# Pacing of the indirect gathers, the order of the small steps and the placing of adjacency units in a four-layer graph network

## The reference

```
h = relu(layernorm(x)); x = x + relu([h, adj @ h] @ W.T + b)                        # layer 0
h = relu(layernorm(x)); x = x + unit_rows(((adj + I) scaled by degrees) @ h @ W.T + b)   # layer 1
h = relu(layernorm(x)); x = x + gru(relu((adj @ h) @ W_msg.T + b_msg), h)           # layer 2
h = relu(layernorm(x))                                                              # layer 3
  z   = leaky_relu(lap_mul(adj, h) @ W1 + b1)
  S   = exp(-0.5 * sqrt(max(|z_i|^2 + |z_j|^2 - 2 z_i.z_j, 0) + 1e-10))
  S   = S on the four most similar j of each row i, else 0
  x   = x + lap_mul(S + adj, h) @ W2 + b2
lap_mul(A, x) = d * (A @ (d * x)),  d = 1 / sqrt(row sums of A)
```

## Time and profile before

| | |
|---|---|
| median of 3 runs | 1389.42 us (1389.1 to 1389.64) |
| the profiled execution, its own time | 1390.72 us |
| its span, first to last instruction | 1388.9 us |
| PE busy | 1312.7 us (95%) |
| DVE busy | 1120.5 us (81%) |
| ACT busy | 867.8 us (62%) |
| POOL busy | 153.1 us (11%) |
| DMA, mean over the span | 222 GB/s |
| granted TensorE clock, mean | 0.98 |

### The profile page before, as it was taken

How to read it: one execution, slowest core, us unless ns; L and a number is a source line. 1 busy time by engine, 2 the same in 40 slices (tenths; PEclk the granted TensorE clock), 3 DMA queues, 4 the chain that set the end, 5 groups by cost and what they waited for, 6 DMA issues and landing times.

```text
span 1388.9 us, 15894 instructions
## 1 busy us (share of the span) xinstructions
PE 1312.7 (95%) x5542; PEld 981.8 (71%) x5542; DVE 1120.5 (81%) x1551; ACT 867.8 (62%) x1302; POOL 153.1 (11%) x178
## 2 busy tenths in 40 slices
PE   7999999999899989999999999999999999869697
PEld 4567888788688767778887778777777775435454
DVE  6898888898998888976658998599999997435455
ACT  5456765447666676765656777566666664547676
POOL 0000110000000000000001000000000001756562
PEclk9999999999999999999999999999999999979899
DMA  9799997558776775666557899201111115769886
GB/s 348 246 328 344 361 340 288 183 186 308 242 239 232 272 278 184 214 210 210 190 183 278 292 318 355 96 1 38 53 53 53 51 44 185 257 227 339 288 312 251
DMA packets 87471, 308.30 MB, mean 222 GB/s; under 512 B 11360, under 2 KB 11488, under 8 KB 87392
## 3 DMA queue, kind: packets, MB, share of 16 engines
q1 hardware_dynamic: 78048, 280.01, 57.6%
q0 software_dynamic: 9344, 27.27, 5.8%
HBM read 303.04 MB, written 4.19 MB: 221 GB/s over the span
## 4 chain that ended last, share of the span: by engine, by line
PE 66%; DVE 27%; issue 3%; ACT 2%; DMA 1%; another core or an unknown queue 1%; ACTq 0%; DVEq 0%
PE ps L507 15%; PE ps L509 15%; PE ps L508 15%; PE ps L512 12%; DVE best_at L1349 9%; DVE rows_T L1345 9%; DVE A_lo L1253 4%; PE ps L579 1%; PE ps L541 1%; PE ps L611 1%; PE ps L613 1%; PE ps L612 1%; DMA ring<-adj_t 1%; PE ps L565 1%
## 5 line engine op out<-in xcount | busy, mean ns | idle before, releaser
L744 ACT ACTIVATE A_hi<-ring 128x1024 fp32r<-128x1024 f32 x399 | 410.1, 1055 | 138.7 <-PE ps L509 82.0
L1253 DVE TENSOR_TENSOR A_lo<-ring,A_hi 128x1024 fp32r<-128x1024 f32 x354 | 416.6, 1217 | 5.9 <-ACT A_hi L744 5.7
L507 PE MATMUL ps<-A_hi,G_odd_hi 128*128 128x512 f32 x602 | 254.2, 422 | 15.8 <-DVE A_lo L1253 9.4
L508 PE MATMUL ps<-A_lo,G_odd_hi 128*128 128x512 f32 x602 | 237.0, 394 | 3.5 <-issue 3.5
L509 PE MATMUL ps<-A_hi,G_odd_lo 128*128 128x512 f32 x602 | 237.4, 394 | 1.9 <-issue 1.9
L507 PE MATMUL ps<-A_hi,G_even_hi 128*128 128x512 f32 x428 | 174.2, 407 | 2.6 <-DVE A_lo L1253 2.6
L744 ACT ACTIVATE scores<-ps,neg_sq 128x1024 f32<-128x1024 f32 x128 | 139.8, 1112 | 53.0 <-PE ps L701 52.4
L509 PE MATMUL ps<-A_hi,G_even_lo 128*128 128x512 f32 x428 | 167.1, 390 | 0.0
L508 PE MATMUL ps<-A_lo,G_even_hi 128*128 128x512 f32 x428 | 166.8, 390 | 0.0
L512 PE MATMUL ps<-ring,G_last 128*128 128x512 f32 x332 | 156.4, 601 | 6.3 <-issue 5.5
L507 PEld LDWEIGHTS ps<-A_hi,G_odd_hi 128*128 128x128 f32 x602 | 114.4, 190 | 56.0 <-issue 20.4
(11 more groups left out here) (156 smaller groups left out, 1650.0 us busy)
## 6 DMA issues: line engine op xcount, KB each, us to landing
ring<-adj_t SPq DMA_DIRECT2D x524, 512.0 KB
row_piece<-adj_rows POOLq DMA_DIRECT2D x32, 512.0 KB, 6.5
X<-x_rows SPq DMA_DIRECT2D x8, 256.0 KB, 7.9
scaled_rows<-G_last POOLq DMA_DIRECT2D x8, 256.0 KB, 2.7
landing<-scaled_rows,best_at POOLq DMA_INDIRECT x128
out_rows<-X SPq DMA_DIRECT2D x8, 256.0 KB, 8.6
pack<-packed SPq DMA_DIRECT2D x1, 836.0 KB, 14.5
pack<-packed SPq DMA_DIRECT2D x1, 192.0 KB, 3.8
```

What stands on the lines that cost most here:

```text
L507: mm(acc, G_hi[odd][:, kb, t, :], hi, start=start, stop=False)
L508: mm(acc, G_hi[odd][:, kb, t, :], lo, start=False, stop=False)
L744: return nc.scalar.activation(out_ap, in_ap, func, **k)
L1253: v_.tensor_tensor(A_lo[:, s, :, :], ring[:, s, :, :], hi, ALU.subtract).then_inc(lower_ready, 1)
```

## The change

Five edits, in `Plan`, the ScalarE, the VectorE and the GpSimd programs:

1. GpSimd no longer waits for `used` ahead of a tile's gathers. `scanned` and `weighted` stay.
2. ScalarE's small steps of block m - 1 stand later: `similarity` behind the third tile of block m instead of the first, `new_roots` behind the fourth instead of the second, `scale_last` behind the first tile of block m + 1 instead of the third of m. At the end of the search they are interleaved accordingly.
3. VectorE's `new_degrees` and `new_inverse` of the first block move one tile later; at the end `new_inverse` of the last but one block moves behind the values of tile 30, and `last_rest` moves from behind the places of tile 31 to behind those of tile 29.
4. Units stand beside seven of eight search tiles (9 to 15, 17 to 23, 25 to 30) instead of three of four (8 to 29): 20 instead of 17 ahead of tile 31, 14 instead of 17 beside tile 31, and the four of the operand block that is scaled last but one come behind those of block 2.
5. ScalarE enters the final stretch when 31 tiles are searched, and waits for the 32nd only at unit 6.

```diff
--- before.py
+++ after.py
@@ -70,10 +70,6 @@
 
 
 LAST_US, NEAR_US, NEAR_FIRST = 1.7, 5.37, 5.0
-
-
-
-UNITS_A_TILE, UNITS_AHEAD = 3.0, 16
 
 
 SPLIT_EVERY = 2
@@ -123,12 +119,16 @@
 
         ended = [b * HALVES + half for b in sorted(range(NB), key=lambda b: self.rank[3, b]) for half in range(HALVES)]
         self.beside = {}
-        for c in range(28):
+        for c in range(24):
             v = self.last_visit(c % 2, ended[c // 2], False)
-            at = 8 + c // 3 * 4 + c % 3
-            self.beside.setdefault(at if at < NT - 2 else NT - 1, []).append(v)
+            at = 9 + c * 8 // 7
+            self.beside.setdefault(min(at, NT - 1), []).append(v)
         for u in ended[:6]:
             self.beside[NT - 1].append(self.last_visit(2, u, False))
+        for c in range(24, 28):
+            v = self.last_visit(c % 2, ended[c // 2], False)
+            at = 9 + c * 8 // 7
+            self.beside.setdefault(min(at, NT - 1), []).append(v)
         self.search_end = len(self.visits)
         for b in range(2):
             for u in ended[-HALVES:]:
@@ -1021,29 +1021,33 @@
                     pair_out(TPB * m + k)
                     if 0 < TPB * m + k <= NB:
                         last_rows_out(TPB * m + k - 1)
-                    if k == 0 and m:
+                    if k == 0 and m > 1:
+                        scale_last(m - 2)
+                    elif k == 2 and m:
                         similarity(m - 1)
-                    elif k == 1 and m:
+                    elif k == 3 and m:
                         new_roots(m - 1)
-                    elif k == 2 and m:
-                        scale_last(m - 1)
             m = NB - 1
             act.wait_ge(negsq_ready, NB)
             pair_out(TPB * m)
+            scale_last(m - 2)
+            pair_out(TPB * m + 1)
+            pair_out(TPB * m + 2)
             similarity(m - 1)
-            pair_out(TPB * m + 1)
+            pair_out(TPB * m + 3)
             new_roots(m - 1)
-            pair_out(TPB * m + 2)
-            pair_out(TPB * m + 3)
             scale_last(m - 1)
             similarity(m)
             new_roots(m)
             scale_last(m)
 
-            act.wait_ge(scanned, NT)
+            act.wait_ge(scanned, NT - 1)
             for v in PLAN.visits[PLAN.search_end:]:
                 if v.split:
                     upper(v)
+                if v.n - PLAN.search_end == 6:
+
+                    act.wait_ge(scanned, NT)
                 if v.n - PLAN.search_end in (6, 10):
                     move_out(4, (v.n - PLAN.search_end) // 4 - 1)
                 elif v.b > 2 and v.u == 3:
@@ -1408,26 +1412,27 @@
                 scan(i)
                 if i % TPB == TPB - 1:
                     clamp(i // TPB)
-                elif i >= TPB and i % TPB == 0:
+                elif i >= TPB and i % TPB == (1 if i < 2 * TPB else 0):
                     new_degrees(i // TPB - 1)
-                elif i >= TPB and i % TPB == 1:
+                elif i >= TPB and i % TPB == (2 if i < 2 * TPB else 1):
                     new_inverse(i // TPB - 1)
 
 
             m = NB - 1
             scan_values(NT - 3)
+            scan_values(NT - 2)
             new_inverse(m - 1)
-            scan_values(NT - 2)
             scan_values(NT - 1)
             clamp(m)
             new_degrees(m)
             new_inverse(m)
-            for i in range(NT - 3, NT):
-                scan_places(i)
+            scan_places(NT - 3)
 
             dve.wait_ge(scanned, NT - 2)
             for k in range(NB):
                 last_rest(k)
+            scan_places(NT - 2)
+            scan_places(NT - 1)
             for v in PLAN.visits[PLAN.search_end:]:
                 if v.split:
                     lower(v)
@@ -1476,8 +1481,6 @@
                 pool.wait_ge(scanned, seek.index(t) + 1)
                 if t >= GSLOTS:
                     pool.wait_ge(weighted, t - GSLOTS + 1)
-                if t >= 2:
-                    pool.wait_ge(used, min(PLAN.search_end + int(UNITS_A_TILE * t) - UNITS_AHEAD, len(PLAN.visits)))
                 for r in range(TOPK):
                     pool.indirect_dma_start(
                         out=landing[:, k, r, :], out_offset=None, in_=scaled_rows,
```

## The result

| | before | changed |
|---|---|---|
| median, runs taken together | 1389.5 us | 1412.9 us (1408.2 to 1416.6) |
| ratio | | 1.016, 95% interval 1.014 to 1.019 |
| the profiled execution, its own time | 1390.7 us | 1413.65 us |
| its span | 1388.9 us | 1411.0 us |
| granted TensorE clock, mean | 0.98 | 0.97 |

The change costs 23 us, 1.6%. The forecast was 1385 and the range ended at 1400.

A forecast was written before the change was run, and what follows sets the result against it. VectorE was taken to bound the search, TensorE its end, with slow stretches during the gathers behind it. Terms -12 + 12 - 4 = -4 us took 1390.7 to 1386.7, less 1.3 over the median: 1385, range 1366 to 1400.

The forecast's parts named there:

- The place that bounds: Behind the search, 1209 to 1231 us: TensorE busy 5.7 of 22 us, almost everybody standing except GpSimd.
- Rival B: Slow stretches behind the search grow because the removed wait was a self-acting brake; +8, 1397 us; chance 0.27.
- Rival A: First slow stretch comes no earlier in TensorE's work, so the search's gain stays: 1377 us, or 1366; chance 0.29.
- Small steps: End of the search: VectorE's waits for scores of tiles 30 and 31 go, 4.7 us; first gather about 1171.
- Units beside seven of eight tiles: Search: still VectorE's bound, 3 units moved forward; first split about 1184 instead of 1196.3, 12 us gained.
- `last_rest`: Subtractions at the search's end move over the first gather: 2 of 4.2 us kept, continuous gathers from about 1173.
- No wait for `used`: First slow stretch: TensorE thins out at 1193, GpSimd goes on to tile 9, until 1223; 12 us handed back.
- 20 us of gathers: Behind the search: TensorE slows after some 16 gathers in a row (20 us), hence at 1193, unit 9 or so.
- the upper bound: First slow stretch: two more tiles of gathers get out, with `weighted` at four, 10 us more.
- Later stretches: Behind 1231 us: a third of GpSimd's breaks go; 4 of TensorE's 16.6 idle us taken as gained.
- Rival B's two signs: First slow stretch lasts past 1230; later breaks have TensorE under half busy for over 8 us each.
- a starved instruction stream: Slow stretch: would stay in its place of TensorE's program, also giving 1377; given 0.03 of the 0.29 chance.

## Why the prediction was wrong

**What was right.** The place that bounds, what happens in it, and the role of the wait: Rival B, "the removed wait was a brake that acts by itself", is what the runs with edit 1 alone and with edits 2 to 5 alone show on the first chip. Of Rival A half came true: its sign, a first stretch that "begins above 1200", did show (1205), and the stretch came "no earlier than before in TensorE's work", behind unit 12. Its price failed, since it took the length as given. That the stretch would take what edits 2 to 5 bring fits their ratio of 1.000 alone, in part by luck: there was little to take. With the wait in place their first split is at 1192.06, 4 us sooner than before, and `lower` of unit 19 at 1235.72, 1.9 us sooner.

**Small steps.** "In the steady search VectorE never waits for ScalarE, so nothing is gained there" was read for gain only. The new place of `similarity` asks for a lead of two tiles, and the rows from which the lead could be read, were taken for a local obstacle of `root`. Measured: -4.7 + 5.5 us; the first gather at 1175.85 instead of 1171.

**Units beside seven of eight tiles.** First split forecast at 1184; measured 1189.98, 6 us sooner than the earlier trace rows and not 12, mostly by the same 5 us. That the search would stay VectorE's held: behind the third block no wait but the last block's own chain remains.

**`last_rest`.** I kept 2 us of the slow gather. The two gathers beside the subtractions took 1.14 and 1.47 us, 0.7 us in all over the usual 0.94: most of the 4.2 us went. The Trainium skill, SBUF — State Buffer, "SBUF: two separate sides", has GpSimd locked out of descriptor writing while VectorE runs an operation in a two-port mode. Whether these subtractions are such, no run here shows; the second gather would fit it (it ends 0.9 us behind the subtractions), the first does not, since it started and ended in 1.14 us between 1172.99 and 1177.89.

**No wait for `used`: the step that failed.** It was sized as 12 us handed back, with TensorE slow from 1193, at unit 9, and GpSimd stopped at tile 10 at 1223. The rule "20 us of gathers" gave the 1193; TensorE became slow at 1205, behind unit 12, 26 us after the gathers had become regular at 1179 (before it took 22). I counted the tiles weighed at 1193 (two), while weighing went on until the machine was slow, and four were weighed by 1202. So `weighted` let 12 tiles go, VectorE's one weighing inside the stretch let out a thirteenth, and the last gather ended at 1243. I had named this as the upper bound ("two more tiles get out", 10 us more) and left it out of the sum. The return to pace, put at 1.5 us behind the stop, took 4 to 7 us. Together: `lower` of unit 13 was still 4.4 us ahead of before (1202.98 against 1207.36) and that of unit 19 was 15.7 behind. The term measured 20 us, not 12, and what it was set against 4 us, not 12; the sum had 0 by then.

**Later stretches.** "I take 4 us of that as gained"; measured 5.6 us lost. The six repeats behind 1231 were read too strongly: in the trace before TensorE stands for more than 2 us at a time in only one of them, between 1294 and 1306; elsewhere its gaps are 1.7 us or less. The changed kernel is under half busy in two windows of 10 us, 1280 to 1290 (3.3 us busy) and 1350 to 1360 (4.7), so of Rival B's two signs the first stretch "past 1230" came and the later ones of "over 8 us each" did not. Rival B had +8 net because it added its loss only to the later stretches and kept 4 us of the first gain; the first stretch, where the brake stood longest open, was the larger term, as its own words said.

**The range** ended at 1400 since Rival B's price left out the upper bound of the first stretch (10 us more). With it B gives 1407 and more.

**Fetches of instructions.** The Trainium skill, Runtime: NRT & Kernel Launch, "Instruction fetch mechanics", states that an engine's sequencer fetches through a DMA queue of its own; a fetch should then show as packets of that queue. Between 1209 and 1250 the changed kernel's trace has none. From 1250 to 1260, once TensorE runs again, it has one; the kernel before has one from 1231 to 1240, once its shorter stretch is over, and on the undisturbed chip one between 1209 and 1220:

```profile
q14 instruction: 1, 0.01, 0.2%
```

The row is the same in each. So the fetch follows the program's progress and comes after the recovery, not ahead of it. This speaks against a starved instruction stream.

## What to carry to other kernels

A wait that never seems to bind on one chip may be the brake that keeps a feedback within bounds on another: before one is removed, ask what stops the engine behind it next, and at what count, with the slow machine's own pace and not the healthy one's. When a step is moved to ask for more lead of another engine, compare the lead that exists at the start; a wait taken away at the end of a pipeline may be paid at its beginning. Where a result hangs on a disturbance that no view explains, time both kernels on several chips, always beside each other.

## What the runs showed of the hardware

- The slow stretches belong to the chip, or to its state at the time, and not to the program. The kernel before took 1385.2 to 1390.7 us in 19 runs on one chip and 1346.2 to 1351.4 on four others, 40 us apart, all but 1 us of it behind the first gather (1175.82 and 1174.82). Which property of the chip it is stays open.
- While they last, TensorE, VectorE, ScalarE and SyncE all but stand and only GpSimd keeps its pace (from 1209 to 1250 in the changed kernel 11.4, 4.8 and 2.5 us busy of 41 for the first three, GpSimd 24.6). The first lasts 21 us where the wait for `used` stops the gathers and 42 where nothing does until `weighted`. At 1.25 us between gathers it begins 29 to 35 us behind the first gather, in five traces, each time at unit 12's last product or the transposes behind it; at 1.39 us, in one trace, not before 60 us. That a spacing above 1.40 us ends them is a conjecture.
- One of the five executions of edit 1 alone took 4675 us. Nothing measured explains it. It is in no ratio; without it their median is 1410.9 us.
